# Scores and exp in two halves, and the V projection spread over the normalisation, in a transformer layer on eight cores

## What is computed

```python
x = x + attn(layernorm(x));  x = x + ffn(layernorm(x))
# attn
q = (x @ wq.T + bq).reshape(B, T, H, D); k, v alike with 4 heads
q = q * cos_q + _rotate_half(q) * sin_q            # k too
scores = einsum('btkgd,bskd->bkgts', qg, k) * scale
scores = scores + tril(ones(T, T))                 # an added 1, not a mask
p = softmax(scores); out = einsum('bkgts,bskd->btkgd', p, v); return out @ wo.T + bo
# ffn
h = gelu(x @ proj1.T + proj1_bias); return h @ proj2.T + proj2_bias
```

## Time and profile before

| | us |
|---|---|
| median of 2 timed runs | 3722.95 (3722.16 to 3723.74) |
| profiled execution, its own time | 3728.9 |
| its span on the slowest core (core 4) | 3727.3 (cores from 3719.6) |
| PE busy | 3103.2 (83%) |
| DVE busy | 1463.2 (39%) |
| ACT busy | 974.1 (26%) |
| phase B0, first to last matmul | 161.9 to about 225.7 |
| phase C, first scores to the drain | 513.8 to about 1540 |

### The profile page before, as it was taken

The page is one execution under the profiler, slowest core; times in us unless marked ns, Lnnn a source line. Parts: engine busy times, 40 slices in busy tenths (PEclk is TensorE's granted clock), DMA queues, the critical chain, the costliest instruction groups (busy, mean ns, idle before and its releaser), DMA issues.

```text
span 3727.3 us, 50953 instructions; the slowest of 8 cores (3719.6 to 3727.3 us)
## 1 busy us (share of the span) xinstructions
PE 3103.2 (83%) x19893; PEld 1643.2 (44%) x20240; DVE 1463.2 (39%) x2429; ACT 974.1 (26%) x1348; POOL 37.7 (1%) x64
## 2 busy tenths in 40 slices
PE   4299976666666666799499999999946999999999
PEld 1144445555555555444144444444412444444444
DVE  2512247777777777422413122231323231322223
ACT  3124445555555555211310100101021001010010
POOL 1000000000000000000000000000000000000000
PEclk8699989999999999999799999999978999999999
DMA  6112200000000000364265655556754555555566
GB/s 206 45 46 80 79 23 2 1 1 2 1 1 2 2 2 2 96 183 145 76 156 147 154 151 150 154 148 156 203 161 105 154 148 157 148 150 155 148 162 188
DMA packets 620060, 381.06 MB, mean 102 GB/s; under 512 B 7089, under 2 KB 605489, under 8 KB 615730
## 3 DMA queue, kind: packets, MB, share of 16 engines
q1 hardware_dynamic: 611762, 344.23, 34.8%
q0 software_dynamic: 8064, 33.56, 2.5%
HBM read 352.60 MB, written 25.17 MB: 101 GB/s over the span
## 4 chain that ended last, share of the span: by engine, by line
PE 77%; ACT 11%; issue 5%; DVE 4%; DMA 3%; ACTq 0%; DVEq 0%; SPq 0%; POOLq 0%
PE psh L921 24%; PE pso L941 24%; ACT xn L527 9%; PE psqk L384 7%; PE scF L475 6%; PE pvps L499 6%; PE pso L631 6%; PE ps_t L485 2%; PE psvt L333 2%; DMA xstg<-xT 1%; DMA xn<-r1T 1%; DVE t L798 1%; DVE qbuf L801 1%; DVE xn L285 1%; DVE xn L282 1%
## 5 line engine op out<-in xcount | busy, mean ns | idle before, releaser
L921 PE MATMUL psh<-qbuf,p1bf 128*128 128x512 bf16 x4014 | 885.8, 380 | 81.1 <-DVE p1bf L864 76.4
L941 PE MATMUL pso<-qbuf,p2bf 128*128 128x512 bf16 x4014 | 880.9, 379 | 16.2 <-ACT qbuf L957 11.9
L921 PEld LDWEIGHTS psh<-qbuf,p1bf 128*128 128x128 bf16 x4096 | 401.9, 98 | 563.9 <-issue 84.0
L527 ACT ACTIVATE xn<-scF 128x128 bf16<-128x128 f32 (+15 forms) x496 | 517.1, 1048 | 438.7 <-PE scF L475 438.7
L941 PEld LDWEIGHTS pso<-qbuf,p2bf 128*128 128x128 bf16 x4096 | 400.2, 98 | 496.8 <-issue 15.4
L475 PE MATMUL scF<-kbuf,qbuf 128*128 128x512 bf16 x897 | 237.3, 381 | 330.0 <-ACT xn L527 307.1
L957 ACT ACTIVATE qbuf<-psh,b1f 128x1024 bf16<-128x1024 f32 x128 | 142.6, 1114 | 1400.1 <-PE psh L921 1400.1
L864 DVE CAST p1bf<-p1stg 128x2048 bf16<-128x2048 f32 x128 | 156.9, 1227 | 692.7 <-PE psh L921 635.6
L898 DVE CAST p2bf<-p2stg 128x2048 bf16<-128x2048 f32 x128 | 157.1, 1227 | 620.5 <-PE pso L941 529.7
L547 DVE COPY xn<-ps_t 128x2048 bf16<-128x2048 bf16 x256 | 313.4, 1224 | 119.4 <-PE ps_t L485 116.2
L485 PEld LDWEIGHTS ps_t<-ident_s,xn 128*128 128x128 bf16 x4096 | 250.7, 98 | 64.6 <-issue 5.0
(11 more groups left out here) (86 smaller groups left out, 1176.8 us busy)
## 6 DMA issues: line engine op xcount, KB each, us to landing
p1stg<-p1T SPq DMA_DIRECT2D x128, 1024.0 KB, 7.2
p2stg<-p2T SPq DMA_DIRECT2D x128, 1024.0 KB, 5.9
wstg<-wqT SPq DMA_DIRECT2D x16, 1024.0 KB, 5.9
wstg<-woT SPq DMA_DIRECT2D x16, 1024.0 KB, 10.4
xblk<-xT SPq DMA_DIRECT2D x16, 1024.0 KB, 6.8
xstg<-xT SPq DMA_DIRECT2D x8, 1024.0 KB, 6.6
xstg<-xT POOLq DMA_DIRECT2D x8, 1024.0 KB, 6.6
r1T<-r1b POOLq DMA_DIRECT2D x16, 512.0 KB, 7.7
```

The source lines that it names most:

```text
L527: last = s.activation(p_sb[u % 3]()[:, lo:hi], scF[:, lo:hi], AF.Exp, bias=f32(bias), scale=f32(D ** -0.5), accum_out=Zp[u % 2][:, ncol:nc ...
L921: ins = t.matmul(psh[hc % 2][:, sl], p1bf[hc % 2][:, c * 128:(c + 1) * 128], xn2[:, c * TH + ns * SWT: c * TH + (ns + 1) * SWT], start=(c ...
L941: ins = t.matmul(pso2[i % 2][:, sl], p2bf[i % 2][:, hc * 128:(hc + 1) * 128], hblk[:, hc * TH + ns * SWT: hc * TH + (ns + 1) * SWT], start ...
```

## The change

It has two parts. **Phase C:** `scF` becomes two PSUM tiles `sc[0]`, `sc[1]` of 1024 columns. PE writes each half with two matmuls of its own and signals after each; the first half of unit u waits for the exp of the first half of u-1, the second for that of the second. ACT takes exp by halves, and a range that crosses column 1024 is cut there; the sums go to one more column of `Zp`. **Phase B0:** PE and ACT skip the barrier ahead of it. The casts of the V weights move from DVE to ACT, into the two `wbf` buffers, four feature chunks at a time. PE works in 8 groups: pass 0 takes token tiles 0 to 7, pass 1 tiles 8 to 15, each over four quarters of the features, with 8 accumulators in all 8 PSUM banks. A group needs only its own four chunks of `xn1` and its own cast. The V weights are loaded once for each pass, so twice. ACT copies the 8 tiles of pass 0 out after the second cast of pass 1. In phase B the first cast's wait is raised by one.

```diff
-            def full_barrier(skip_sync=False):
+            def full_barrier(skip_sync=False, skip=()):
...
-            full_barrier(skip_sync=True)
+            full_barrier(skip_sync=True, skip=("tensor", "scalar"))
...
+                    CPS = (128 * C) // (128 * KVD)
+                    NQP = NCC // CPS
+                    TPG = min(8, NT)
+                    NPASS = NT // TPG
+                    NL = NPASS * NQP
...
                     def phB0_sync(sync):
-                        for q in range(NQ):
+                        for q in range(NL):
+                            qq = q % NQP
                             p.w(sync, "s_pool", bB0["s_pool"] + q - 1)
...
-                    def phB0_cast(v):
-                        for q in range(NQ):
-                            p.w(v, f"ld_w{q % 2}", 16 * (q // 2 + 1))
-                            p.inc(v.tensor_copy(
-                                wvbf[:, q * CPS * KVD:(q + 1) * CPS * KVD],
-                                wstg[q % 2][:, 0:CPS * KVD]), "s_pool")
-                    block.vector(phB0_cast)
+                    def phB0_sc(s):
+                        def cast(i):
+                            p.w(s, f"ld_w{i % 2}", 16 * (i // 2 + 1))
+                            if i >= 2:
+                                p.w(s, "s_pe", bB0["s_pe"] + i - 1)
+                            p.inc(s.activation(wbf[i % 2][:, 0:CPS * KVD],
+                                               wstg[i % 2][:, 0:CPS * KVD],
+                                               AF.Identity, bias=f32(0.0)),
+                                  "s_pool")
+
+                        def evac(j):
+                            p.w(s, "s_pe",
+                                bB0["s_pe"] + (j // TPG + 1) * NQP)
+                            p.inc(s.activation(vTb[:, j * KVD:(j + 1) * KVD],
+                                               psvt[j % TPG][:], AF.Identity,
+                                               bias=f32(0.0)), "s_act")
+                        for hv in range(NPASS):
+                            for qq in range(NQP):
+                                cast(hv * NQP + qq)
+                                if qq == 1 and hv >= 1:
+                                    for j in range((hv - 1) * TPG, hv * TPG):
+                                        evac(j)
+                        for j in range((NPASS - 1) * TPG, NPASS * TPG):
+                            evac(j)
...
                     def phB0_pe(t):
-                        p.w(t, "s_dve", bB0["s_dve"])
-                        p.w(t, "s_pool", bB0["s_pool"] + NQ)
-                        for j in range(NT):
-                            p.w(t, "s_act", bB0["s_act"] + j - 1)
-                            for c in range(NCC):
-                                t.matmul(psvt[j % 2][:],
...
+                        for g in range(NL):
+                            hv, qq = divmod(g, NQP)
+                            p.w(t, "s_pool", bB0["s_pool"] + g + 1)
+                            p.w(t, "s_dve",
+                                bA["s_dve"] + 5 + 2 * (CPS * qq + CPS - 1))
+                            if qq == 0 and hv > 0:
+                                p.w(t, "s_act", bB0["s_act"] + hv * TPG)
+                            for j in range(hv * TPG, (hv + 1) * TPG):
+                                for ci in range(CPS):
+                                    c = qq * CPS + ci
+                                    ins = t.matmul(
+                                        psvt[j % TPG][:],
...
+                            if qq == NQP - 1:
+                                for j in range(hv * TPG, (hv + 1) * TPG):
+                                    ins = t.matmul(psvt[j % TPG][:], ones1[:],
+                                                   bvr_bf[:], start=False,
+                                                   stop=True)
+                            p.inc(ins, "s_pe")
...
-                            p.w(v, "s_pe", bB["s_pe"] + oc - 1)
+                            p.w(v, "s_pe", bB["s_pe"] + max(oc - 1, 0))
...
-                scF = esC.enter_context(nc.psum_tensor("scF", [128, T], F32))
+                sc = [esC.enter_context(
+                    nc.psum_tensor(f"sc{i}", [128, T // 2], F32))
+                    for i in range(2)]
...
-                            p.w(t, "s_act_exp", u)
-                            for n2 in range(2 * NS2):
...
+                            for sh in range(2):
+                                p.w(t, "s_act_exp", 2 * u - 1 + sh)
+                                for n2 in range(NS2):
+                                    o = kv * T + sh * (T // 2) + n2 * SWH
+                                    ins = t.matmul(
+                                        sc[sh][:, n2 * SWH:(n2 + 1) * SWH],
+                                        lhs, kbuf[:, o:o + SWH],
+                                        start=True, stop=True)
+                                p.inc(ins, "s_pe_sc")
...
+                        ncol = 0
+                        for sh in range(2):
+                            h0, h1 = sh * (T // 2), (sh + 1) * (T // 2)
+                            p.w(s, "s_pe_sc", 2 * u + 1 + sh)
+                            if sh == 0:
+                                p.w(s, "s_dve_p", u - 1)
+                                p.w(s, "s_pe_tr", u - 2)
+                            last = None
+                            for (lo, hi, bias) in rs:
+                                il, ih = max(lo, h0), min(hi, h1)
+                                if il >= ih:
+                                    continue
+                                acc = Zp[u % 2][:, ncol:ncol + 1]
+                                ncol += 1
+                                last = s.activation(
+                                    p_sb[u % 3]()[:, il:ih],
+                                    sc[sh][:, il - h0:ih - h0], AF.Exp,
+                                    bias=f32(bias), scale=f32(D ** -0.5),
+                                    accum_out=acc)
+                            p.inc(last, "s_act_exp")
...
-                            p.w(v, "s_act_exp", u + 1)
+                            p.w(v, "s_act_exp", 2 * u + 2)
```

More of the change, by code:

```diff
@@ L339, in build_nc @@
-                    block.tensor(phB0_pe)
-                    def phB0_act(s):
-                        for j in range(NT):
-                            p.w(s, "s_pe", bB0["s_pe"] + j + 1)
-                            p.inc(s.activation(vTb[:, j * KVD:(j + 1) * KVD],
-                                               psvt[j % 2][:], AF.Identity,
-                                               bias=f32(0.0)), "s_act")
-                    block.scalar(phB0_act)
+                    def phB0_sc(s):
[21 more added lines that the diff above has]
+                            evac(j)
@@ new lines, in build_nc @@
+                    block.scalar(phB0_sc)
+                    def phB0_pe(t):
+                        for g in range(NL):
[10 more added lines that the diff above has]
+                                        psvt[j % TPG][:],
+                                        xn1[:, c * T + j * 128:
+                                            c * T + (j + 1) * 128],
+                                        wbf[g % 2][:, ci * KVD:(ci + 1) * KVD],
+                                        start=(c == 0), stop=False)
+                            if qq == NQP - 1:
[4 more added lines that the diff above has]
+                            p.inc(ins, "s_pe")
@@ L471, in phC_pe @@
                             lhs = qbuf[:, hh * T + tt * 128:hh * T + (tt + 1) * 128]
-                            p.w(t, "s_act_exp", u)
-                            for n2 in range(2 * NS2):
-                                o = kv * T + n2 * SWH
-                                ins = t.matmul(
-                                    scF[:, n2 * SWH:(n2 + 1) * SWH],
-                                    lhs, kbuf[:, o:o + SWH],
-                                    start=True, stop=True)
-                            p.inc(ins, "s_pe_sc")
+                            for sh in range(2):
[7 more added lines that the diff above has]
+                                p.inc(ins, "s_pe_sc")
                         if 2 <= u < NU + 2:
@@ L521, in phC_act @@
                         rs = ranges_of(tt)
-                        p.w(s, "s_pe_sc", u + 1)
-                        p.w(s, "s_dve_p", u - 1)
-                        p.w(s, "s_pe_tr", u - 2)
-                        last = None
-                        for ncol, (lo, hi, bias) in enumerate(rs):
-                            last = s.activation(
-                                p_sb[u % 3]()[:, lo:hi],
-                                scF[:, lo:hi], AF.Exp,
-                                bias=f32(bias), scale=f32(D ** -0.5),
-                                accum_out=Zp[u % 2][:, ncol:ncol + 1])
-                        p.inc(last, "s_act_exp")
+                        ncol = 0
```

(4 more changed lines are left out.)

24 lines of the change are left out of this document (9 added, 15 removed).

## The result

The change makes the kernel faster: the median is 3596.14 us, and the ratio to the kernel before is 0.9647 (95% interval 0.9634 to 0.9659), about 131 us. Predicted were 3601 us and a gain of 122. (Some executions of either kernel are disturbed on one die; all ratios here are of undisturbed runs, and rows come from cores of an undisturbed die.)

A forecast was written before the change was run, and what follows sets the result against it. Attention was taken as bound by the hand-over between PE and ACT. Gains of 101 us there and 21 us in the V projection, 122 off 3722.95, gave 3601 us, range 3570 to 3650.

The forecast's parts named there:

- The loop: Attention: DVE's path through single `ps_t` from one P times V block to the next, 14.16 us per four units.
- The row-sum term: Attention: time from DVE's copy of `ps_t` after the block to its row sum, taken as 1.18 us.
- PE's longest wait in attention: Attention: sign set beforehand; the prediction is wrong if this wait is still the one for exp.
- the 2 us subtracted for token tile 0 and the ends: Attention: less gain expected there, so 103 us became 101 us.
- ACT is ahead by 0.6 us: Attention: ACT's way to the next block ends about 930.7, DVE frees `ps_t` at 931.35, so DVE sets the end.
- 8 bias matmuls in a row: V projection: 0.3 us taken for each, 2.4 us a pass; bounds 0.217 and 0.41 each.
- The slow start of pass 1: V projection: PE starts the second pass at the lower clock after idling, adding 1.8 us.
- the slow start of phase B: Start of phase B, after the V projection: PE again starts from idle, adding 1.8 us.
- Common steps unchanged: Attention rival: steps without the block stay at 3.49 us, or little better; 3630 to 3690 us, chance 0.18.
- Halves gain nothing: Attention rival: PE's rigid order keeps four units near 15.8 us, only the V part gains; 3702 us, chance 0.04.
- DVE as plain bound: Attention rival: DVE runs at 12.5 us per four units; 3489 us, chance 0.08 for that or near it.
- Clock: Attention rival: PE's clock falls to the lower level, up to 4048 us if throughout; chance 0.03.

The follow-up runs named there:

- experiment 4: Changed kernel with P times V cut into four pieces of 16 matmuls, one per unit: median 3492.81 us, ratio 0.9374 to the kernel before.
- experiment 6: Changed kernel with one more ACTIVATE of 128 x 256 per unit on ACT: ratio 0.9643 to the kernel before, attention 921.8 us.
- experiment 7: Changed kernel with one more copy of 128 x 512 per unit on DVE: ratio 0.9717 to the kernel before, attention 946.8 us.
- experiment 10: Changed kernel with exp of the diagonal block as its own range and DVE's row sum removed, P times V still whole: ratio 0.9522 to the kernel before.
- experiment 1: Kernel before with only the attention halves, V projection as it was: ratio 0.9706, attention 921.5 us.
- experiment 3: Kernel before with scores and exp cut in halves, but waits kept whole so nothing overlaps: ratio 1.0079, attention 1058.3 us.
- experiment 5: Kernel before, scores and exp whole, with only P times V cut into four pieces: ratio 0.9686, attention 910.1 us.
- experiment 9: Changed kernel with P times V in four pieces, V copies ahead of the cast, and DVE's row sum removed: median 3398.7 us, ratio 0.9104.

## Why the prediction was right

**The bound.** "DVE has the most work. But it can't run at 12.5, because `ps_t` stays a single tile": right. Experiments 4, 6, 7 and 10 show it from four sides. The loop came out at 14.16 and was measured at 14.13. The row-sum term was 1.18 for a measured 1.15, the others were within 0.02. One of the signs that the prediction set itself, PE's longest wait in attention, came out as a tie (74.0 us for exp, 73.2 for DVE's copy), and by itself would have decided nothing. It was badly chosen: a total adds up waits that delay nobody. The experiments decide.

**The size.** The gain of a group was right: 1.61 us by the rounded 14.2, and 1.64 measured in the mean (15.81 to 14.17). The term that failed is the 2 us subtracted for token tile 0 and the ends. Tile 0 did gain less, 1.23 us a group (15.34 to 14.11). But the stretches ahead of the first block and behind the last, which I had put down as giving less, gave 4.3 us. So attention gained 105.8 and not 101. (That 63 times 1.68, as the expectation of experiment 1 has it, gives the same 105.8 is chance: 1.68 is the difference of the medians, and there are 62 such groups at 1.64.)

**ACT.** "ACT is ahead by 0.6 us" was too little; it was ahead by 1.0 (experiment 6). The rows of the changed kernel show where the 0.4 lay. The copy of `pvps` counts 0.48 us from its start to that of the next exp, not the 0.60 for which its row shows it busy, and the three exps before the block take 2.15, 2.22 and 2.27 us (core 5, from 900.51 on), not 2.31, in part since the met waits cost nothing (experiment 3). That is 0.12 + 0.29 = 0.41.

**V projection.** The steps came as described. Against 97.9 us to phase B the median is 95.9. The terms that missed: 8 bias matmuls in a row take 1.90 us from the first start to the last end, 0.217 each, the lower bound and not 0.3 (0.7 us a pass); 8 copies take 4.0 us and not 4.9, since one follows the other after 0.48 us though each is busy for about 0.60 (0.9 us, and twice). The slow start of pass 1 cost more than I had, 9.6 us for its first group against 7.07, 2.5 instead of 1.8. Against it stands the last group of pass 0, 8.7 us on core 5 where I had 6.9: its clock fell. I had that as a bound of the range only. It fell there on cores 1 and 5 only (97.3 us to phase B on both); on the other six (95.4 to 96.1) it fell in group 2, where it costs nothing (last section). Then 1.8 us was charged to the slow start of phase B; K and Q took 1.0 more. Five cores of the kernel before, at 286.8 to 287.1, start slow there too, unlike core 4 with 285.3, from which I read that it doesn't. Together 24 us instead of 21. Most of that miss, 2.1 us, lies in the kernel before: core 4, on which I had worked, takes 405.9 us for the two stretches, the median core 408.0. In the executions of experiments 1, 3 and 5, where this part is as before, K and Q take 285.5 in the median, and against these the gain is 22.5 to 22.8 us, so that more than 1 us of the 24 is luck of these two executions.

On the copies: the Trainium skill, "ScalarE: Activation LUTs", section "What ACT_TABLE_LOAD costs", says that ACTIVATEs one behind the other overlap by about 93 ns. The first two copies here agree: the second starts 0.48 us after the first, which is busy for 0.58, an overlap of 0.10. Further on in the row of eight the records overlap by more, up to 0.17, while the starts stay 0.48 apart.

**The rivals.** Common steps unchanged: no, 3.12 for 3.49. Halves gain nothing: no, though experiment 3 shows that without overlap they lose 0.8%. DVE as plain bound: not in this kernel; it becomes so in experiment 4, at 3492.8 us, 4 us from the 3489 that the rival was given. Clock: 1.00 for 901 of the 922 us of attention, at 739.9 / 901 = 82% busy (busy times of the records, drains included). What the Trainium skill tells of 512-column matmuls that cycle through banks, a clock that swings between its levels ("TensorE: Matmul & The Clock Gate", section "A second HAM failure mode: psum-queue depth-cycling"), was not seen here.

**A trap in the profile.** The chain gives ACT's exp the largest part of attention:

```profile
by line: ACT xn L566 40.5%; PE pvps L529 26.3%; issue 14.0%; DVE xn L586 7.2%; PE ps_t L515 6.2%; PE sc L505 5.2%; ACT qbuf L545 3.5%; ACTq L38 1.1%; DVEq L38 0.1%
```

(shares of the stretch 899 to 916, by line). Experiment 6 put 0.6 us more on ACT's way to the block and nothing moved. Two ways through the loop were 1.0 us apart in 14.1, and a chain that is followed back through inferred releasers names one of them, not the one that counts.

## What to carry to other kernels

When two engines hand a buffer back and forth, follow the loop from its rarest large piece of work and write down every term between two passes; what is in the loop once, twice or four times decides what an edit is worth. Look for the large piece first: cutting a block of matmuls that sat between two uses of a single buffer into four gave more than double buffering the scores did, for no added instruction. The two together, with the V projection and one DVE instruction less, gave 9% (experiment 9). To tell which of two close engines is the bound, add work to each: the chain could not say it, 0.3 us on ACT and 0.2 us on DVE did. And take the time from the start of one instruction to the start of the next, not the time for which its row shows it busy: that error stood here in the copies to `vTb` and in the copy of `pvps`, with 0.12 us for each copy.

## What the runs showed of the hardware that I had not expected

The granted clock fell while PE had a group of matmuls to run without a pause, and where it fell decided what it cost. Core 0 of the changed kernel in pass 0 of the V projection (timeline):

```profile
130.87 8.75 PE L362 MATMUL psvt<-wbf,xn 128*128 128x512 bf16 x32 [3.57 <-DVE xn L288]
...
141.50 7.07 PE L362 MATMUL psvt<-wbf,xn 128*128 128x512 bf16 x32 [1.88 <-DVE xn L288]
```

Group 2 is slow, 8.75 us for 32 matmuls: the granted clock is 1.00 in the pause up to 130.8, 0.50 from 130.9 to 134.3 and 1.00 again behind that. But the next four chunks of `xn1` come only 10.6 us after the group began, and nothing is lost. On core 5 group 2 has 1.00 and 7.07 us, and the clock falls in the last group, 1.3 us after its start, and the group takes 8.75 us, behind which everything waits. Both falls come in or at the start of a group behind an idle time of 3.57 us (before 130.87 and before 149.39). But so does group 2 of core 5, and there the clock stays at 1.00: that idle time alone does not decide it, and what does is not shown. I did not try other gaps.

In experiment 4, in which DVE hardly waits for another engine (0.8 us in all for the transposes), now and then a unit takes 3.48 us instead of 3.13, with an idle time of 0.46 us, where it is 0.1 otherwise, between two small DVE instructions that depend on each other:

```profile
1021.64 0.16 DVE L609 RECIPROCAL rz<-Zs 128x1 f32<-128x1 f32 x1 [0.46 <-DVE Zs L605]
```

What it is has not been tried.
